# Where the expert biases are added in a routed feed-forward stage, and one set of piece buffers in place of two

## The reference, cut to what matters

```python
for i in range(E):                                   # E = 8 experts
    h = jnp.einsum('bsd,df->bsf', x, w1[i]) + b1[i]  # 256 -> 2048
    a, g = jnp.split(h, 2, axis=-1)
    y = jnp.einsum('bsh,hd->bsd', a * jax.nn.sigmoid(g), w2[i]) + b2[i]   # 1024 -> 256
    out = out + jnp.where((top1 == i)[..., None], y, 0.0)
```

## Time and profile before

| | |
|---|---|
| median of three runs | 436.2 us |
| profiled execution, its own time | 437.39 us |
| its span in the trace | 435.6 us |
| PE busy | 92% of the span |
| DVE, ACT, POOL busy | 56%, 50%, 29% |
| granted TensorE clock, mean | 0.976 |

### The profile page before, as it was taken

The page is one execution under the profiler, slowest core; times in us unless marked ns, Lnnn a source line. Parts: engine busy times, 40 slices in busy tenths (PEclk is TensorE's granted clock), DMA queues, the critical chain, the costliest instruction groups (busy, mean ns, idle before and its releaser), DMA issues.

```text
span 435.6 us, 8490 instructions
## 1 busy us (share of the span) xinstructions
PE 400.9 (92%) x3018; PEld 266.2 (61%) x3026; DVE 242.8 (56%) x659; ACT 216.9 (50%) x406; POOL 125.5 (29%) x149
## 2 busy tenths in 40 slices
PE   6969899899898889969999999999999999999992
PEld 2535444455465455735777767677777777777671
DVE  3859965677776844775245543455434544354421
ACT  2315468465556556103644464466546657465630
POOL 5259050021010010357655311111111111055532
PEclk9989999899999999996999999999999999999998
DMA  6565495261011652023955520950009300001101
GB/s 216 119 169 127 107 184 184 55 144 50 15 50 50 220 219 98 36 72 97 303 196 162 189 74 0 362 219 2 1 17 410 156 1 2 2 35 53 49 38 48
DMA packets 26023, 49.32 MB, mean 113 GB/s; under 512 B 7490, under 2 KB 17726, under 8 KB 25982
## 3 DMA queue, kind: packets, MB, share of 16 engines
q1 hardware_dynamic: 21778, 40.53, 28.6%
q0 software_dynamic: 2688, 7.26, 4.9%
q10 hardware_dynamic: 1516, 0.99, 0.9%
HBM read 34.41 MB, written 6.93 MB: 95 GB/s over the span
## 4 chain that ended last, share of the span: by engine, by line
PE 78%; DVE 9%; ACT 3%; issue 3%; SPq 3%; DMA 2%; ACTq 1%; POOL 0%; DVEq 0%
PE bank L1237 22%; PE bank L1274 12%; PE bank L1229 9%; PE bank L1265 5%; PE bank L1068 4%; PE bank L979 4%; PE bank L989 3%; PE bank L928 3%; DVE row_max L1602 2%; PE bank L865 2%; DMA x_sb<-in_x_dram 2%; PE bank L889 2%; PE bank L967 2%; PE bank L1043 2%; ACT probs L1360 2%
## 5 line engine op out<-in xcount | busy, mean ns | idle before, releaser
L1237 PEld LDWEIGHTS bank<-slot_rows,w_now 128*128 128x128 f32 x832 | 100.6, 192 | 5.2 <-issue 1.6
L1237 PE MATMUL bank<-slot_rows,w_now 128*128 128x128 f32 x832 | 101.9, 276 | 0.7 <-ACT slot_rows L1436 0.7
L1870 DVE SCALAR_TENSOR_TENSOR act_ut<-bank,b_of,gate 128x128 f32<-128x128 f32 x104 | 31.7, 346 | 73.0 <-ACT gate L1475 73.0
L819 POOL COPY piece_w<-w_sb 128x1536 f32 x23 | 33.6, 1466 | 129.4 <-PE bank L1265 118.5
L1602 DVE TENSOR_REDUCE row_max<-bank 128x3 f32<-128x462 f32 (+1 forms) x96 | 52.9, 578 | 17.2 <-PE bank L928 16.8
L1451 ACT ACTIVATE w_now<-w_sb 128x1024 f32 x52 | 54.9, 1057 | 12.4 <-issue 12.0
L1360 ACT ACTIVATE probs<-bank 128x512 f32<-128x512 f32 x80 | 46.0, 597 | 27.0 <-PE bank L967 18.1
L1274 PE MATMUL bank<-w_sb,act_ut 128*128 x208 | 56.0, 393 | 0.0
L1475 ACT ACTIVATE gate<-bank,b_of 128x128 f32<-128x128 f32 x104 | 32.5, 367 | 41.3 <-PE bank L1237 37.7
L1274 PEld LDWEIGHTS bank<-w_sb,act_ut 128*128 128x128 f32 x208 | 35.4, 190 | 17.0 <-issue 12.7
L699 POOL TENSOR_SCALAR var<-mv 128x1 f32<-128x1 f32 (+1 forms) x20 | 4.6, 232 | 128.8 <-DVE mv L1639 105.1
(11 more groups left out here) (192 smaller groups left out, 536.7 us busy)
## 6 DMA issues: line engine op xcount, KB each, us to landing
w_sb<-in_weights_dram SPq DMA_DIRECT2D x32, 768.0 KB, 7.0
q_stack<-q_split SPq DMA_DIRECT2D x18, 256.0 KB, 4.7
rows<-row_buf SPq DMA_DIRECT2D x17, 256.0 KB, 2.7
x_sb<-in_x_dram SPq DMA_DIRECT2D x4, 512.0 KB, 5.5
k_stack<-k_split SPq DMA_DIRECT2D x12, 77.0 KB
q_stack<-q_split ACTq DMA_DIRECT2D x6, 128.0 KB, 2.8
q_stack<-q_split SPq DMA_DIRECT2D x6, 128.0 KB, 2.5
ctx_sb<-in_ctx_t_dram SPq DMA_DIRECT2D x1, 320.0 KB, 7.4
```

What stands on the lines that cost most here:

```text
L819: pool.tensor_copy(piece_w[:, k % 2, c, :], piece_weights(k, experts[at])).then_inc(pieces_pool, 1)
L1237: ins = pe.matmul(h_ps[j % RING][:, P * m:P * (m + 1)], w1_now[:, whole_count(n) % 2, k, P * m:P * (m + 1)], slot_rows[:, tile_at(n), P * ...
```

## The change

**Biases.** In quarters two to four a mixed tile gets no bias matmul. `b1` is also stored to DRAM as plain float32 rows (`b1_rows`), and the SP queue loads, per piece, one row of 512 values to 32 partitions (`load_bias`: four DMAs for each of 15 mixed tiles, 64 KB each, into `bias_in[:, m]`). SP reads the piece's expert from `tile_expert` first (20 loads into registers, once). A new DVE instruction (`bias`) adds the bank and `bias_in` into `hidden` (128x512, SBUF), and `gates` and `gated` of the tile read `hidden`. In the first quarter mixed tiles keep the matmuls for `b1` and `b2`. Whole tiles lose the `b2` matmul of the first quarter; GpSimd adds `b2` to their `slot_rows` in the second quarter (`add_b2`, 13 instructions of 128x256, from `b2_sb`, which one DMA of 1 MB fills), and DVE's `add_y` of that quarter waits for it (`b2_added`).

**Pieces.** One set of `piece_w1` (1024 columns) and `piece_w2` (512 columns) takes the place of the two sets. The copy of `w1` for mixed tile `k` waits for the upward product of `k - 1`, the copy of `w2` for the downward product of `k - 1`; both are issued in the step of a mixed tile, `w2` of that tile itself and `w1` of the next one (for the first mixed tile of a quarter: in the first step of that quarter, where before its copy stood in the step of the last mixed tile).

**The diff, cut to its core:**

```diff
+        def w2_due(n):
+            return [mixed_count(n) - 1] if n > MIXED_AT[0] and mixed(n) else []
+        def w1_due(n):
+            return [k for k in range(1, QUARTERS * MIXED_TILES)
+                    if n == max(mixed_at(k - 1), k // MIXED_TILES * SLOT_TILES)]
+        def w1_of_piece(engine, k, expert):
+            engine.wait_ge(s_quarter[k // MIXED_TILES], 16 * EXPERTS)
+            if k >= 1:
+                engine.wait_ge(h_ready, mixed_at(k - 1) + 1)
+        def w2_of_piece(engine, k, expert):
+            if k >= 1:
+                engine.wait_ge(y_ready, downs_before(mixed_at(k - 1)) + 1)
...
             # TensorE, up(n)
+                if n >= RING and mixed(n - RING) and n - RING >= SLOT_TILES:
+                    pe.wait_ge(biased, mixed_count(n - RING) - MIXED_TILES)
+                    if q == 0:
+                        for c in range(PIECES):
+                            pe.matmul(h_ps[j % RING][PIECE * c:PIECE * (c + 1), :], expert_rows(piece_at(k_mixed, c), PIECE),
+                                      b_split[:, 0:2 * HQ], start=True, stop=False, skip_group_check=True)
...
             # TensorE, down(n) of a whole tile
-                    if first:
-                        pe.matmul(y_ps[d % RING][:, 0:DIM], expert_rows(tile_at(n), P), b2_rows, start=True, stop=False)
...
             # VectorE
+            def bias(n):
+                k = mixed_count(n) - 1
+                q, m = divmod(k, MIXED_TILES)
+                dve.wait_ge(h_ready, n + 1)
+                dve.wait_ge(mixed_ready, k)
+                dve.wait_ge(bias_arrived[m], 16 * PIECES * q)
+                dve.tensor_tensor(hidden[:, :], h_ps[n % SLOT_TILES % RING][:, :], bias_in[:, m, :], ALU.add).then_inc(biased, 1)
...
             # GpSimd, in step j + 19
+            def add_b2(j):
+                pool.wait_ge(y_added, downs_before(j) + 1)
+                y = slot_rows[:, at, DIM:2 * DIM]
+                pool.tensor_tensor(y, y, b2_sb[:, bass.ds(expert, 1), :].rearrange("p o n -> p (o n)"), ALU.add).then_inc(b2_added, 1)
...
             # SP queue
+            for q in range(1, QUARTERS):
+                if q >= 2:
+                    sp.wait_ge(y_ready, max(downs_before(n) for n in range(SLOT_TILES * (q - 2), SLOT_TILES * (q - 1)) if not mixed(n)) + 1)
+                    load_experts(q, 0, EXPERTS)
+                for m in range(MIXED_TILES):
+                    load_bias(MIXED_TILES * q + m)
```

More of the change, by code:

```diff
@@ L322, in build @@
         bias_loaded = sem("bias_loaded")
+        b2_loaded = sem("b2_loaded")
+        b2_added = sem("b2_added")
+        biased = sem("biased")
+        bias_arrived = [sem(f"bias_arrived{m}") for m in range(MIXED_TILES)]
         b1_turned = sem("b1_turned")
@@ L846, in _ @@
                     gather(n + GATHERS)
-                for k in pieces_due(n, 0):
-                    if k < MIXED_TILES:
-                        copy_piece(k, 2)
-                    copy_piece(k, 3)
+                for k in w2_due(n):
+                    for c in pool_pieces(k):
+                        copy_w2(k, c)
+                for k in w1_due(n):
+                    for c in pool_pieces(k):
+                        copy_w1(k, c)
+                if SLOT_TILES + 1 <= n <= 2 * SLOT_TILES and not mixed(n - SLOT_TILES - 1):
+                    add_b2(n - SLOT_TILES - 1)
                 for i in sum(downs(n - 2), []):
@@ L1270, in down @@
                     pe.wait_ge(u_ready, whole_count(n))
-                    if first:
-                        pe.matmul(y_ps[d % RING][:, 0:DIM], expert_rows(tile_at(n), P), b2_rows, start=True, stop=False)
                     for k in range(KH):
                         ins = pe.matmul(y_ps[d % RING][:, 0:DIM], act_ut[:, whole_count(n) % RING, k, :],
-                                        expert_weights(n, at + DIM * k, at + DIM * (k + 1)), start=(k == 0 and not first),
-                                        stop=(k == KH - 1))
+                                        expert_weights(n, at + DIM * k, at + DIM * (k + 1)), start=(k == 0), stop=(k == KH - 1))
                 ins.then_inc(y_ready, 1)
@@ L1465, in gates @@
                     wait_gated(act, n - 2)
+                if mixed(n) and n >= SLOT_TILES:
+                    act.wait_ge(biased, mixed_count(n) - MIXED_TILES)
+                    act.activation(gate[:, n % 2, :, :].rearrange("p m n -> p (m n)"), hidden[:, HQ:2 * HQ],
+                                   ACT.Sigmoid).then_inc(gate_ready, 1)
+                    return
                 act.wait_ge(h_ready, n + 1)
@@ L1877, in add_y, with copy_w1, copy_w2, copy_due @@
                 dve.wait_ge(y_ready, d + 1)
+                if SLOT_TILES <= n < 2 * SLOT_TILES and not mixed(n):
+                    dve.wait_ge(b2_added, whole_count(n - SLOT_TILES))
                 y = slot_rows[:, tile_at(n), DIM:2 * DIM]
                 dve.tensor_tensor(y, y_ps[d % RING][:, 0:DIM], y, ALU.add).then_inc(y_added, 1)
-            def copy_piece(k, c):
+            def copy_w1(k, c):
                 at = piece_at(k, c)
-                wait_piece(dve, k)
                 if k < MIXED_TILES:
                     load_expert(at)
-                dve.tensor_copy(piece_w[:, k % 2, c, :], piece_weights(k, experts[at])).then_inc(pieces_dve, 1)
+                dve.tensor_copy(piece_w1[:, c, :], w1_of_piece(dve, k, experts[at])).then_inc(w1_dve, 1)
+            def copy_w2(k, c):
+                dve.tensor_copy(piece_w2[:, c, :], w2_of_piece(dve, k, experts[piece_at(k, c)])).then_inc(w2_dve, 1)
+            def copy_due(n, c):
+                for k in w2_due(n):
+                    copy_w2(k, c)
+                for k in w1_due(n):
+                    copy_w1(k, c)
             dve.wait_ge(s_b1, 16)
             place_b1(0)
-            for k in range(2):
+            for copy in (copy_w1, copy_w2):
                 for c in range(2):
-                    copy_piece(k, c)
+                    copy(0, c)
             for n in range(QUARTERS * SLOT_TILES):
@@ L1896, in _ @@
                     add_y(i)
-                for k in pieces_due(n, 1):
-                    copy_piece(k, 1)
+                if mixed(n) and n >= SLOT_TILES:
+                    bias(n)
+                copy_due(n - 1, 1)
                 gated(n)
@@ L1901, in _ @@
                     add_y(i)
[L1902 to L1903 removed]
+                copy_due(n, 0)
                 if n in (6, 9, 12):
```

120 lines of the change are left out of this document (70 added, 50 removed).

## The result

| | before | after |
|---|---|---|
| median | 436.24 us (4 executions) | 423.75 us (423.15 to 424.12, 4 executions) |
| profiled execution, its own time and its span | 437.39, 435.6 us | 424.12, 422.0 us |
| feed-forward stage in the trace | 221.92 us | 210.38 us |

The changed kernel is faster, at a ratio of 0.9722 (95%: 0.9695 to 0.9748).

What follows compares the result with a forecast made beforehand. TensorE's back-to-back matmuls were taken to bound the feed-forward stage. Removing 4.8 us (`b1` of mixed tiles) and 5.2 us (`b2` of whole tiles), 10.0 us, from 436.2 gave 426.2 us, range 424.3 to 431.0.

Steps and rivals of the forecast that it cites:

- The frame: Feed-forward stage: TensorE's matmuls run without a gap, so array time taken out comes off in full, 10.0 us.
- B: Bias matmuls: only streaming time goes, changes of columns and rows keep their price elsewhere; gain 5.9 us, chance 0.14.
- D: Transposes of mixed tiles: PE waits for the longer addition chain; 3.8 us slower, at 440.0 us, chance 0.06.
- E: Bias matmuls held no time because loads behind them could not come earlier; no change, 436.2 us, chance 0.06.
- the term for `b1`: Mixed tiles, quarters two to four: 15 bias groups at 0.32 us go, 4.8 us, bounds 3.2 to 5.8.
- The term for `b2`: Whole tiles, first quarter: 13 bias matmuls at 0.21 us plus 0.19 behind each go, 5.2 us, bounds 2.7 to 6.1.
- What would show it: Signs expected in the new trace, such as mixed tiles 0.32 us closer and L1331 at 0.87 us in the first quarter.
- The cover for the longer way to the transpose: Mixed tiles: DVE's addition delays the multiplication to 1.75 us, transpose still at 2.64; cost 0, 0.9 us spare.
- Rival C: Quarter two and quarter starts: GpSimd and DVE block each other, costing up to 3.9 us; gain 6.1 us, chance 0.12.
- The first mixed tile of a quarter: Later piece copies by DVE leave some 0.4 us spare; otherwise each of three quarters loses up to 0.3 us.
- SP and the DMAs: Bias-row loads hold SP until 262 to 272 us, before the third quarter's weights are due at 276; cost 0.

Runs made afterwards that it cites:

- no_b2: The kernel before without the 13 matmuls that add `b2` of whole tiles, that bias left out: median 430.98 us against 436.43, stage 217.86 us.
- add_x2: The changed kernel with DVE's bias addition of mixed tiles done twice, the surplus result unread: median 425.34 us, stage 210.17 us.
- add_x3: The changed kernel with DVE's bias addition of mixed tiles done three times, the surplus results unread: median 429.95 us, stage 216.46 us.
- all_off: The changed kernel with no bias matmul left, first-quarter `b1` by DMA and DVE, all `b2` by GpSimd: median 422.61 us, stage 207.14 us.

## Why the prediction was right or wrong

**The frame was right.** The stage was a row of matmuls without a gap, and what was taken out of it came off the time in full. Rivals B, D and E are out: L1285 did not grow, PE stood idle ahead of no transpose, and the time changed.

**The step that failed is the term for `b1`,** 4.8 us with a high end of 5.8. It measured 6.6. The prediction took the group's piece of the chain, "since the chain's piece begins and ends where L1265 ends and L1229 begins". That piece is right (15 x 0.32 to 0.33 = 4.9). But the product behind it was slower by 0.14 us for the change of rows, in 12 of 15 tiles, and this was left out. For `b2` of whole tiles the prediction did count the product behind (0.19 us), because the trace had the same four matmuls with and without a bias ahead. For `b1` no mixed tile stood without one, and the working took the absence of such a row for the absence of a price. The high end was no bound either: it held the bias matmul's own duration, and the price stood outside it. The trace of before had a sign of it: the loads stood idle for 0.23 us behind the bias.

**The term for `b2` was right:** 13 x 0.40 = 5.2 us, measured 5.2 in the changed kernel, and 0.405 a tile in `no_b2`.

**The range** had a second fault. It was worked out from array time alone, while the start of the stage lay between 201.7 and 205.2 us in kernels with the same or nearly the same code ahead of it. Its low end should have had one or two us for that. With the right term for `b1` (11.8 for both) the forecast would have been 424.4, still 0.65 above the median. The stage's own 11.5 us, taken from 436.2, give 424.7, which lies inside the range. So the mis-sized term accounts for 1.5 us of the 2.5 that were missed (1.8 less the 0.3 that went the other way), and the last 1.0 us, which put the median below 424.3, is of the size of the spread ahead of the stage; no run shows it to be the change's work.

**What would show it, point by point.** L1281 is the only 24-row `b1` group and ends with the first quarter (20 matmuls, 80 before). The way between two mixed tiles in the later quarters is 0.46 us shorter (0.32 + 0.14), not 0.32. L1331 stands at 0.87 in the first quarter, and the way between mixed tiles there went from 10.57 to 9.76 us, the 0.8 foreseen. PE is never idle ahead of L1301, though one pair and the four matmuls behind it take 0.09 us longer. The additions in detail (min/median/max in ns; compare):

```profile
L1931 DVE TENSOR_TENSOR hidden<-bank,bias_in x15: 690/691/693, 266.8 to 402.0; 128x512 f32<-128x512 f32 x15
...
L881 POOL TENSOR_TENSOR slot_rows<-slot_rows,b_sb x13: 723/730/917, 253.8 to 302.9; 128x256 f32<-128x256 f32 x13
```

DVE's addition took 0.69 us (0.64 from the slope), within its bounds. GpSimd's took 0.73 (0.73 to 0.97 foreseen), its copy of 1024 columns 1.04 (0.98 foreseen).

**The cover for the longer way to the transpose** was as worked out: where nothing disturbs it the multiplication ends 1.75 us after the upward product, and the transposes' load comes at about 2.57. The prediction had 0.9 us to spare, and 0.8 were there. `add_x2` used up 0.6 of them at no cost, and `add_x3`, with 1.2, went past them by the 0.41 us that each tile then cost.

**Rival C** had the right mechanism and the wrong price. The prediction held against it that GpSimd's copy has just ended at 1.3 us. But GpSimd goes on to the next instruction at once, and it is the next one that wins the race by 0.02 us, every time. What made it harmless is the spare time: 0.55 us late against 0.8 spare in four tiles. In the fifth it was 0.86 late, and 0.1 us was lost.

**The first mixed tile of a quarter, SP and the DMAs** cost nothing, as said. The upward product of the third quarter's first mixed tile begins at 315.58, where the piece ahead of it ends. That this place has little room shows in `all_off`, which lost 0.33 us there. SP's first loads of bias rows, with the reads between them, last from 247.8 to 269.3 us and end inside the 262 to 272 foreseen, and no engine waits for a row. GpSimd waited once for `b2_sb`, for 2.0 us, and no piece of the chain waits for that.

## What to carry to other kernels

Where TensorE is the bound, a small matmul of another row count costs more than its own place in the chain: look at the load and the product behind it too, and at whether the two counts could be made equal. Filling 24 rows up to 128 with zeros in one operand, with every matmul kept, gave three quarters of what the whole change gave (8.6 of 11.5 us), and is the cheaper edit to try first. When a range is made, put the spread of what stands ahead of the changed stage into it.

## What the runs showed of the hardware

- A change between 24 and 128 rows, at the same number of columns, costs 0.10 us on the way in and 0.14 us (32 columns, 512 wide) or 0.19 us (128 columns, 256 wide) on the way out; ahead of the 16 of a mixed downward product it is 0.11.
- A change between 32 and 128 columns has a price of the same kind: 1.87 for 1.73, 1.98 for 1.78 and 1.06 for 0.87 us. Both changes at one place cost one price.
- A DVE multiplication of two SBUF operands (0.43 us alone) waited for the whole GpSimd instruction that had begun 0.02 or 0.03 us before it, up to 1.03 us, and ended 0.28 us behind it.
- DVE additions of 128x512 that follow each other begin 0.60 us apart, though each takes 0.69 in the trace.
- DVE's addition of a bank and SBUF took 0.69 us for 128x512, while the multiplication from SBUF took 0.43 for 128x256. The copies took 0.68 us (128x1024) and 0.42 (128x512) on DVE, 1.04 and 0.61 on GpSimd.
